# Cross attention: who transposes the low halves of the softmax weights

## The reference, cut to what matters

```python
def _L1_xattn_ref(q, k, v, wq, wk, wv, wo):     # q = layernorm(x), k = v = ctx_1024
    qh = (q @ wq.T).reshape(B, Sq, 16, 64).transpose(0, 2, 1, 3)
    kh = (k @ wk.T).reshape(B, Sk, 16, 64).transpose(0, 2, 1, 3)
    vh = (v @ wv.T).reshape(B, Sk, 16, 64).transpose(0, 2, 1, 3)
    scores = jnp.einsum('bhqd,bhkd->bhqk', qh, kh) / 8.0
    attn = jax.nn.softmax(scores, axis=-1)
    ctx = jnp.einsum('bhqk,bhkd->bhqd', attn, vh)
    return ctx.transpose(0, 2, 1, 3).reshape(B, Sq, 1024) @ wo.T
```

## Time and profile before

| | us |
|---|---|
| median of 3 runs | 3616.16 (3609.43 to 3617.14) |
| the profiled execution | 3610.95 |
| its span | 3609.2 |
| cross attention, from the first to the last `ca_pt` transpose issued | 1864.2 to 3407.3 |

### The profile page before, as it was taken

One profiled execution on the slowest core, in us unless ns is written; L12 is line 12 of the kernel. 1 busy time (PEld: TensorE's weight loads), 2 busy tenths in 40 slices (PEclk: granted clock), 3 DMA queues, 4 the chain that ended last, 5 costly groups with the idle time before them and its releaser, 6 DMA issues. The chain is left out here.

```text
span 3609.2 us, 78473 instructions
## 1 busy us (share of the span) xinstructions
PE 3069.9 (85%) x30984; PEld 1833.0 (51%) x31124; DVE 2697.0 (75%) x4017; ACT 2354.9 (65%) x4397; POOL 1062.7 (29%) x1854
## 2 busy tenths in 40 slices
PE   6999989968998944999958898998899989999824
PEld 3747474745665633444435554555555555555411
DVE  4848483767887855344459998889888989899688
ACT  3838383766876634333349988779877888788534
POOL 2232323056346334233322222222222222222122
PEclk9999999989998977999989999999999999999956
DMA  4050505074375175244489999999999999999843
GB/s 154 27 158 18 174 2 151 13 266 120 134 229 169 53 246 202 82 122 121 115 217 192 194 190 203 190 201 198 209 184 194 200 208 188 192 203 192 155 160 126
DMA packets 1308095, 572.96 MB, mean 159 GB/s; under 512 B 1144146, under 2 KB 1230802, under 8 KB 1305172
## 3 DMA queue, kind: packets, MB, share of 16 engines
q1 hardware_dynamic: 1303700, 551.16, 69.4%
q0 software_dynamic: 4032, 16.78, 1.2%
HBM read 174.19 MB, written 109.45 MB: 79 GB/s over the span
## 5 line engine op out<-in xcount | busy, mean ns | idle before, releaser
L2309 DVE TENSOR_REDUCE ca_neg_max<-banks 128x1 f32<-128x1024 f32 x512 | 624.1, 1219 | 82.6 <-PE banks L2087 81.0
L2317 DVE SCALAR_TENSOR_TENSOR ca_halves<-ca_probs,ca_inv,ca_halves 128x1024 f16<-128x1024 f32 x512 | 655.5, 1280 | 39.1 <-ACT ca_halves L2243 29.9
L2235 ACT ACTIVATE ca_probs<-banks,ca_neg_max 128x1024 f32<-128x1024 f32 x512 | 570.5, 1114 | 80.4 <-DVE ca_neg_max L2309 77.5
L2243 ACT ACTIVATE ca_halves<-ca_probs,ca_inv 128x1024 f16<-128x1024 f32 x512 | 587.1, 1147 | 15.8 <-DMA ca_pt<-ca_halves 14.9
L2053 POOL TENSOR_SCALAR ca_inv<-ca_total 128x1 f32<-128x1 f32 x512 | 98.4, 192 | 1153.2 <-ACT ca_probs L2235 1153.2
L2087 PE MATMUL banks<-ca_kt,ca_qt 64*128 64x512 f16 x3072 | 381.0, 381 | 34.3 <-ACT ca_probs L2235 32.8
L2109 PE MATMUL banks<-ca_pt,ca_v 128*64 128x256 f16 x6144 | 387.7, 276 | 16.4 <-DMA ca_pt<-ca_halves 16.2
L2109 PEld LDWEIGHTS banks<-ca_pt,ca_v 128*64 128x64 f16 x6144 | 319.0, 110 | 108.5 <-issue 88.9
L2056 POOL TENSOR_TENSOR ca_inv<-ca_inv,ca_minus_one 128x1 f32<-128x1 f32 x512 | 281.6, 550 | 42.6
L2087 PEld LDWEIGHTS banks<-ca_kt,ca_qt 64*128 64x128 f16 x3072 | 131.3, 95 | 224.6 <-issue 80.8
L2068 PE MATMUL banks<-ca_ct,ca_w 128*128 128x512 f16 x768 | 179.0, 383 | 38.2 <-DMA ca_ct<-ctx_part 23.6
(11 more groups left out here) (306 smaller groups left out, 5737.2 us busy)
## 6 DMA issues: line engine op xcount, KB each, us to landing
ca_w<-ca_w_parts SPq DMA_DIRECT2D x20, 768.0 KB, 5.3
wa_v<-v_rows SPq DMA_DIRECT2D x44, 264.0 KB, 4.6
v_rows<-wa_v_stage SPq DMA_DIRECT2D x32, 264.0 KB, 2.2
wa_x<-in_x SPq DMA_DIRECT2D x32, 256.0 KB, 4.8
wa_ring<-in_x SPq DMA_DIRECT2D x32, 256.0 KB, 3.6
x_after_window_attention<-wa_ring SPq DMA_DIRECT2D x32, 256.0 KB, 3.2
ba_tokens<-wa_tok_turned SPq DMA_DIRECT2D x32, 256.0 KB, 3.6
ba_xt<-ba_tokens SPq DMA_DIRECT2D x32, 256.0 KB, 7.6
```

What stands on the lines that cost most here:

```text
L2235: act.activation(probs[:, slot, :], scores(i), ACT.Exp, bias=neg_max[:, slot:slot + 1], accum_out=total[:, slot:slot + 1]).then_inc(exped, 1)
L2243: act.activation(halves[:, i % HALF_SLOTS, 0, :], probs[:, slot, :], ACT.Copy, scale=inv[:, slot:slot + 1]).then_inc(split_hi, 1)
L2309: dve.tensor_reduce(out=neg_max[:, slot:slot + 1], in_=scores(i), axis=X_AXIS, op=ALU.max, negate=True).then_inc(maxed, 1)
L2317: dve.scalar_tensor_tensor(out=halves[:, i % HALF_SLOTS, 1, :], in0=probs[:, slot, :], scalar=inv[:, slot:slot + 1], in1=halves[:, i % HAL ...
```

## The change

Nothing is flipped any more: the DMA transposes both halves of each of the 512 units. TensorE's transposes, ScalarE's copies and the waits for them go; steps that held a flip hold no work beside. Nothing else is moved.

```diff
-        flip_at = {step: 2 * (step - 1) for step in range(2, STEPS)
-                   if not any(step in busy for busy in (qk_at, v_at, tile_at, partly_at))}
-        flipped_units = set(flip_at.values())
...
                             sp.wait_ge(split_lo, i + 1)
-                            parts = 1 if i in flipped_units else 2
-                            sp.dma_start_transpose(pt[:, step % 4, h, 0:parts * NT, :],
-                                                   halves[:, i % HALF_SLOTS, 0:parts, :].rearrange("p q s -> p (q s)")
+                            sp.dma_start_transpose(pt[:, step % 4, h, :, :],
+                                                   halves[:, i % HALF_SLOTS, :, :].rearrange("p q s -> p (q s)")
                                                    ).then_inc(turned[i % HALF_SLOTS], 16)
...
                             pe.wait_ge(turned[i % HALF_SLOTS], turned_by(i))
-                        if flips_until(4 * g + 3):
-                            pe.wait_ge(low_placed, flips_until(4 * g + 3))
...
-                    flips = sum(1 for at in flip_at if at < step)
-                    if flips:
-                        pe.wait_ge(low_placed, flips)
...
-                def flip_low(i):
-
-                    bank = psum[:, SPARE, :].bitcast(F16)
-                    pe.wait_ge(split_lo, i + 1)
-                    for kb in range(NT):
-                        last = pe.transpose(bank[:, kb * P:(kb + 1) * P],
-                                            halves[:, i % HALF_SLOTS, 1, kb * P:(kb + 1) * P], consts.ident_h[:, :])
-                    last.then_inc(low_flipped, 1)
-
                 def beside(step):
-                    if step in flip_at:
-                        spare_free(step)
-                        flip_low(flip_at[step])
...
                 def high_item(step):
-                    if step in flip_at:
-                        i = flip_at[step]
-                        act.wait_ge(low_flipped, flips_until(i))
-                        if step >= 5:
-                            act.wait_ge(weighted, (step - 5) // 2 + 1)
-                        act.activation(pt[:, (step - 1) % 4, 0, NT:2 * NT, :],
-                                       psum[:, SPARE, :].bitcast(F16).rearrange("p (k c) -> p k c", c=P),
-                                       ACT.Copy).then_inc(low_placed, 1)
...
                     dve.wait_ge(split_hi, i + 1)
-                    if i - HALF_SLOTS in flipped_units:
-                        dve.wait_ge(low_flipped, flips_until(i - HALF_SLOTS))
```

More of the change, by code:

```diff
@@ L1953, in cross_attention @@
         partly_at = {STEPS - 10 + t: t for t in range(NT)}
-        flip_at = {step: 2 * (step - 1) for step in range(2, STEPS)
-                   if not any(step in busy for busy in (qk_at, v_at, tile_at, partly_at))}
-        flipped_units = set(flip_at.values())
-        low_flipped, low_placed = sem("ca_low_flipped"), sem("ca_low_placed")
-        def flips_until(unit):
-            return sum(1 for u in flipped_units if u <= unit)
         store_at = {step + 2: tile for step, tile in tile_at.items()}
```

## The result

The changed kernel took 3632.18 us (median of 5 runs, 3630.61 to 3638.1); the kernel before, beside it, 3611.21 (3605.95 to 3617.14). The ratio is 1.0054 [1.0041, 1.0068]: slower by 21 us, more than the 0.2% that can be told, and a little past the upper end of the range.

What follows compares the result with a forecast made beforehand. Regular cross-attention turns were taken as bound by a loop through ScalarE's flip evictions, batch ends by the DMA queue. Terms -12.0 and +9.9 summed to -2 us: 3609 profiled, 3614 for the median of runs, range 3600 to 3631.

Steps and rivals of the forecast that it cites:

- The loop: Cross attention's regular turns: ScalarE's two flip evictions are on the 45.24 us loop; without them engines could do 43.83.
- TensorE's part: Removing 36 times eight transposes, 22 us of TensorE's time, was claimed worth 0 by itself.
- ScalarE's part: Removing 36 evictions of 1.02 us gives at most 2 x 0.70 = 1.41 us per regular turn.
- The queue in regular turns: DMA queue needs 44.5 us per regular turn, about as tight as the loop; 44.24 taken, gain 12.0 over twelve turns.
- the upper bound: Longest regular turn if the DMA queue sets it: 45.6 us, from today's queue row of 38.64 + 1.5 + 5.5.
- The clock: First batch end: TensorE's matmuls behind a wait take 2.77 instead of 1.50 us; price left as it is.
- The batch ends: Three batch ends: the queue ends last, halves made full add 3 x 1.1 = 3.3 us each, 9.9 us later in all.
- The slower one: Queue takes over: regular turns at 45.6 (+4.8), batch ends +12, together +16.8, 3633; slower side's chance 0.23.
- The faster rival: Queue keeps up everywhere: regular turns 43.83 (-16.9), batch ends lose only 1.0 each (+3.0), 3602; chance 0.27.

Runs made afterwards that it cites:

- f1: Changed kernel, but low halves of 35 of the 36 formerly flipped units transposed by nobody, so no more DMA than before; 3592.96 us, ratio 0.9941 to the kernel before.
- f5: Changed kernel without the 16 weight loads after turn 3 (later pairs of heads use the first four pairs' weights); 3612.23 us in a single run.
- m2: Kernel before plus four groups of eight full transposes ahead of cross attention, a weight load inside the third and fourth; 3721.05 us, single run, bursts included.
- m1: Kernel before plus groups of eight full transposes, then of halves, ahead of cross attention with nothing else running; 3758.28 us, single run, bursts included.
- f7: Kernel before with flips kept only in the four steps of each batch end (12 of 36), none in regular turns; 3626.97 us, ratio 1.0028.
- f2: Kernel before with flips kept, copies going to a scratch tile, and the DMA transposing both halves of every unit as well; 3641.07 us, ratio 1.0074.
- h2: Kernel before without each regular turn's first flip, and with a batch end's eight token loads two steps earlier; 3617.78 us, ratio 1.0005 to the kernel before.
- n1: Changed kernel with each 768 KB weight load cut into three of 256 KB, issued in three steps of a turn; 3644.62 us, ratio 1.0089 to the kernel before.

## Why the prediction was wrong

- **The loop: right.** The evictions ended last; without them the engines make a turn in 43.92 (forecast 43.83) as long as the queue keeps up (f1, f5). TensorE's part at 0 fits: ScalarE's part alone was forecast to give what f1 shows.
- **The queue in regular turns: the step that failed.** It said 16 x 2.75 + 0.54 = 44.5 and took 44.24, a gain of 1.0. The 2.75 was nearly right: 2.69 in line. The term that was mis-sized is the 0.54: it is the weight load's issue on SyncE, not its work. The load costs 2.7 (m2, measured alone), and without it the turn is 43.9 (f5). So the sum is 16 x 2.69 + 2.7 = 45.7, an estimate from two runs, against the engines' 43.9; measured were 46.2. With 2.7 for the load, the prediction's own sum is 16 x 2.75 + 2.7 = 46.7, slower than before, and the loop's gain could not have been had. The twelve regular turns gave +9.9 where -12.0 was taken: 21.9 of the 27.7 by which the stage's 25.7 missed the forecast of -2. Even the upper bound, 45.6, was too low, though it was called too slow a bound. Its row had the load's work in it, which the 0.54 left out; that it lies so near 45.7 is partly luck, since two pauses of the queue, of 0.4 and 0.8, are in that row too.
- **The clock: a term put at nothing.** The prediction left the price of TensorE's slow matmuls behind a wait "as it is". It grew: the granted clock of turn 7 fell from 0.93 to 0.88, and regular turns, which had none of it before, now have it too (turn 4, above). Turn 4 is 2.2 above f1's 43.92 without a landing that ScalarE waits for; if turns 13 and 21 lost as much by it, that would be an estimated 0.6 in the mean of eleven, about what is missing between 45.7 and 46.2. That this fills it is not shown, because a longer turn also lets the queue catch up.
- **The batch ends: right in kind, a little small in size.** TensorE's longest wait became 8.19 (7 to 9 was forecast), turns 7, 15 and 23 grew to 55.4 to 56.1 (53 to 56), +15.6, and turns 6, 14 and 22 gave 1.2 back: 14.3 against 9.9. Alone, a half made full costs 1.1 (m1), as taken; the sum counted three of them at each end, and four would be 4.4 of the 4.8 measured. f7 shows that those four flips alone bring turns 7, 15 and 23 back to 50.57 (50.66 before). Turn 30's 1.6 is in no term of the sum; of all kernels here only the changed one and f2 have it (49.16), the others 47.3 to 47.54.
- **The rivals.** The slower one's place and sign were right: from 45.24 on the queue takes over, in both places. That its total, 3633, is nearly the time measured is luck: it is +16.8 on a median of 3616.16, where the change measured +21 on 3611.21, and in other parts, with regular turns at 45.6 and no term for turn 30. The faster rival's regular turns are what f5 shows, and only without loads; its small loss at the batch ends came in no run that makes those four halves full. The Trainium skill's 261 GB/s for a DMA transpose (DMA: Bandwidth & Descriptors, Latency and other measured facts), which the page gives for a layout that is not contiguous, stood beside that rival. It is not reached here: alone a full one of 0.52 MB in 2.49 is 211 GB/s, and in line 195.

Still open: why a transpose in line takes 2.69 when the same alone takes 2.49, the 0.5 between 45.7 and 46.2, turn 30, and the mechanism of h2. The sum holds for the mean turn and not for each (45.37 to 47.63): in turn 4 the queue has caught up before the load, in n1 it is behind in all of them, and the means are 46.20 and 46.29.

## What to carry to other kernels

Price a transfer in a full queue by what it adds to a group of others there; the length of its issue instruction does not tell it, as 0.54 against 2.7. Before taking work off an engine's loop onto a DMA queue, add up the queue's whole turn, loads included, and compare it with the loop that will be left, not with today's. Where both come out close, move a part: with one flip of two the loop took 44.60 and the queue still fit in nine turns of eleven.

## What the runs showed of the hardware

- A 128x2048 f16 transpose costs less than two of 128x1024 (2.49 against 2 x 1.37), so making a half full adds 1.1, not another 1.37.
- A plain load of 768 KB adds 2.7 to a group of eight transposes that takes 21.86 (m2). In the kernel the regular turn is as long when SyncE issues the load whole (46.20), when GpSimd does (46.65) and when it comes in three pieces (46.29), and 43.9 without it (f5).
- The waits cost twice: behind 8.19 of idle time TensorE's next 24 and 12 matmuls took 2.77 and 2.61 instead of 1.50 and 1.47, and the granted clock of the turn was 0.88 (0.93 before), between the levels of 1.2 and 2.4 GHz. In regular turns 3 and 4 it was 0.97 and 0.96, where it was 1.00 before, and a projection's 48 matmuls took 5.02 instead of 2.85.
